# Splitting the projection weights on two engines, and other orders of the lists, in a fused attention and Mamba kernel

## The reference, cut to what matters

```python
# layer 0: cross-attention, 16 heads of 16
q, k, v = relu(x @ Wq + bq), relu(c @ Wk + bk), relu(c @ Wv + bv)
scores = where(mask_of_the_query_row, q k^T / sqrt(16), 1e-9)
x = layernorm(softmax(scores) @ v + x) * gamma + beta
# layer 1, first half: a Mamba block
z, xBC, dt = split(rmsnorm(x) @ in_proj_w)        # 512, 768 and 8 columns
xBC = silu(conv_b + 4 taps along the sequence)    # gives xh (512), B (128), C (128)
dt = softplus(dt + dt_bias); decay = exp(-exp(A_log) * dt)
y = linear recurrence over 128 rows in 8 heads + D_skip * xh
x = x + rmsnorm(y * silu(z)) @ out_proj_w
# layer 1, second half: cross-attention with 8 heads of 32 on the same context
out = x + softmax(layernorm(x) @ Wq1 (c @ Wk1)^T / sqrt(32)) @ (c @ Wv1) @ Wo
```

## Time and profile before

| what | value |
|---|---|
| median of 3 runs | 1336.95 us (1336.31 to 1337.32) |
| the profiled execution | 1338.95 us, of which the span of its trace 1337.2 us |
| mean granted clock of PE | 0.99 |
| PE, DVE, ACT, POOL busy | 97, 90, 85, 69% of the span |
| DMA | 87.00 MB, mean 65 GB/s |
| chain that ended last | PE 87%, DVE 4%, ACT 4%, issue 2% |

### The profile page before, as it was taken

The page is one execution under the profiler, slowest core; times in us unless marked ns, Lnnn a source line. Parts: engine busy times, 40 slices in busy tenths (PEclk is TensorE's granted clock), DMA queues, the critical chain, the costliest instruction groups (busy, mean ns, idle before and its releaser), DMA issues.

```text
span 1337.2 us, 43414 instructions
## 1 busy us (share of the span) xinstructions
PE 1291.6 (97%) x15624; PEld 1148.0 (86%) x15624; DVE 1208.1 (90%) x3056; ACT 1130.8 (85%) x3407; POOL 928.7 (69%) x1200
## 2 busy tenths in 40 slices
PE   5879999999999999999999999999999999999987
PEld 4668889988888998889998889989888898888875
DVE  6789999999999999999999999999999989999982
ACT  5658989888889988888988888998888898888875
POOL 3366777777767777777777776777777777766774
PEclk9889999999999999999999999999999999999999
DMA  6102221212221112222121222211222221111110
GB/s 203 40 34 72 69 77 38 70 56 69 77 77 62 52 49 69 77 77 77 38 66 60 69 77 77 61 53 50 69 77 77 71 71 34 62 56 57 49 57 25
DMA packets 41283, 87.00 MB, mean 65 GB/s; under 512 B 5744, under 2 KB 10992, under 8 KB 41072
## 3 DMA queue, kind: packets, MB, share of 16 engines
q1 hardware_dynamic: 40208, 83.81, 19.7%
...
q10 hardware_dynamic: 864, 0.42, 0.1%
...
## 4 chain that ended last, share of the span: by engine, by line
PE 87%; DVE 4%; ACT 4%; issue 2%; DMA 1%; POOL 1%; SPq 1%; ACTq 0%; DVEq 0%
PE bank L319 26%; PE bank L422 10%; PE bank L550 6%; PE bank L412 5%; PE bank L379 5%; PE bank L533 5%; PE bank L436 4%; PE bank L564 4%; PE bank L669 4%; PE bank L360 3%; PE bank L604 3%; PE bank L625 2%; PE bank L654 2%; PE bank L470 2%; PE bank L416 1%
## 5 line engine op out<-in xcount | busy, mean ns | idle before, releaser
L951 DVE SCALAR_TENSOR_TENSOR ACC<-bank,cw,ACC 128x250 f32<-128x250 f32 (+2 forms) x576 | 264.1, 462 | 5.9 <-ACT ACC L1535 3.3
L319 PE MATMUL bank<-xnT,wnl 128*128 128x256 f32 x640 | 201.6, 315 | 3.3 <-DVE xnL L883 2.3
L1622 ACT ACTIVATE PC<-bank,stc 128x128 f32<-128x128 f32 x512 | 182.5, 389 | 7.7 <-DVE stc L1068 4.3
L319 PE MATMUL bank<-xnL,wnh 128*128 128x256 f32 x640 | 180.3, 282 | 0.0
L319 PE MATMUL bank<-xnT,wnh 128*128 128x256 f32 x640 | 179.8, 281 | 0.0
L800 DVE TENSOR_REDUCE sta<-bank 128x4 f32<-128x512 f32 x256 | 163.7, 673 | 7.8 <-PE bank L379 7.5
L977 DVE TENSOR_TENSOR_SCAN L<-DB,id 128x1024 f32<-128x1024 f32 x64 | 146.8, 2293 | 0.8 <-DMA DB<-dec_scratch 0.8
L319 PEld LDWEIGHTS bank<-xnT,wnl 128*128 128x128 f32 x640 | 121.9, 190 | 26.0 <-issue 17.6
L1437 ACT ACTIVATE PTA<-bank 128x512 f32<-128x512 f32 x256 | 133.3, 628 | 9.0 <-PE bank L416 5.3
L1916 POOL TENSOR_TENSOR PC<-PC,stc 128x512 f32<-128x512 f32 x128 | 132.1, 1042 | 11.3 <-DVE stc L1075 11.3
L319 PEld LDWEIGHTS bank<-xnL,wnh 128*128 128x128 f32 x640 | 122.4, 191 | 0.0
...
## 6 DMA issues: line engine op xcount, KB each, us to landing
...
```

The lines of the kernel that those rows point to most:

```text
L319: mm = e.matmul(t[:, c0:c0 + T], wt[:, k, m:m + 128], x[:, k, :], start=(n == 0), stop=(n == 5))
L951: e.scalar_tensor_tensor(out=w, in0=t[:, 0:T].rearrange("p (b t) -> p b t", b=NB)[:, :, 0:125 + k], scalar=cw[:, c, k:k + 1], in1=w, op0=A ...
L1622: op = e.activation(PC[n % 4][:, p, :], t[:, p * 128:(p + 1) * 128], ACT.Exp, bias=stc[g % 4][:, 4 * i + p:4 * i + p + 1], accum_out=stc[g ...
```

## The change

1. `weights()` becomes `weights(k)`. The half k=0 is done by DVE before `rc(0, 0)`, all of it. For k=1, ACT makes the two wide copies to `wnh` in `eA(0, 4)`; DVE does the rest before `rc(0, 1)`, and waits for ACT's by a new semaphore `z_nk`.
2. ACT's copies `wk1h`, `wv1h` go from `eA(0, 4)` to `n1(0, 1)`, behind `wouth`; POOL's `wk1l`, `wv1l` go from the second call of `xr` to the third (`xr(1, 0)`).
3. The five lists have other orders, in head, loop and tail, and `USES` has other banks. The loops hold the same calls as before; they start at another place of the cycle, and the heads and tails are longer or shorter to match.

```diff
-                    if ns == 0:
-                        weights()
+                    if ns < 2:
+                        weights(ns)
...
-            def weights():
-                e.wait_ge(z_sq, 4)
+            def weights(k):
+                w, wz = pc[:, 4 + k:5 + k], pc[:, 18 + k:19 + k]
                 e.wait_ge(d_win, 32)
-                for k in range(2):
-                    w, wz = pc[:, 4 + k:5 + k], pc[:, 18 + k:19 + k]
+                if k == 0:
+                    e.wait_ge(z_sq, 4)
                     e.tensor_scalar(wnh[:, k, 0:512], stage[k][:, 0:512], wz, None, ALU.mult)
-                    e.tensor_scalar(wnh[:, k, 512:1280], stage[k][:, 512:1280], w, None, ALU.mult).then_inc(z_nh, 1)
...
+                    e.tensor_scalar(wnh[:, k, 512:1280], stage[k][:, 512:1280], w, None, ALU.mult)
+                e.tensor_scalar(wdt[:, k, 1, 0:8], stage[k][:, 1280:1288], w, None, ALU.mult)
+                e.tensor_scalar(wdt[:, k, 0, 0:8], stage[k][:, 1280:1288], w, None, ALU.mult).then_inc(z_nh, 1)
+                e.tensor_scalar(wdt[:, k, 1, 8:16], stage[k][:, 1280:1288], 0.0, None, ALU.mult)
+                e.wait_ge(z_nh, k + 1)
+                if k == 1:
+                    e.wait_ge(z_nk, 2)
+                for lo, hi, c in ((0, 512, wz), (512, 1280, w)):
+                    e.scalar_tensor_tensor(out=wnl[:, k, lo:hi], in0=stage[k][:, lo:hi], scalar=c, in1=wnh[:, k, lo:hi].bitcast(F32),
+                                           op0=ALU.mult, op1=ALU.subtract)
...
                     if n == 4:
-                        e.wait_ge(d_late, 48)
-                        for hi, w in ((wk1h, w1[0]), (wv1h, w1[1])):
-                            e.activation(hi[:, :, :], w, ACT.Copy).then_inc(z_1h, 1)
+                        e.wait_ge(d_win, 32)
+                        for lo, hi, c in ((0, 512, 18), (512, 1280, 4)):
+                            e.activation(wnh[:, 1, lo:hi], stage[1][:, lo:hi], ACT.Copy, scale=pc[:, c + 1:c + 2]).then_inc(z_nk, 1)
...
                             e.activation(wouth[:, k, :], ws[k], ACT.Copy, scale=pc[:, 6 + k:7 + k]).then_inc(z_wo2, 1)
+                        e.wait_ge(d_late, 48)
+                        for hi, w in ((wk1h, w1[0]), (wv1h, w1[1])):
+                            e.activation(hi[:, :, :], w, ACT.Copy).then_inc(z_1h, 1)
...
-                    if ns == 1:
+                    if ns == 2:
```

PE's head up to the first input projection, before and after:

```diff
-            q(0, 0); q(0, 1); k(0, 0); k(0, 1); v(0, 0); sA(0, 0); q(1, 0); q(1, 1); sA(0, 1); tn(0, 0); k(1, 0); v(1, 0)
-            sT(0, 0); k(1, 1); av(0, 0); av(0, 1); av(0, 2); av(0, 3); tn(0, 1); ot(0, 0); q(2, 0); sT(0, 1); q(2, 1)
-            av(0, 4); av(0, 5); av(0, 6); av(0, 7); sA(1, 0); ot(0, 1); sA(1, 1); k(2, 0); v(2, 0); nt(0, 0); cp(0, 0)
...
+            q(0, 0); q(0, 1); k(0, 0); v(0, 0); k(0, 1); sA(0, 0); q(1, 0); q(1, 1); sA(0, 1); k(1, 0); tn(0, 0); v(1, 0)
+            sT(0, 0); av(0, 0); tn(0, 1); av(0, 1); av(0, 2); av(0, 3); k(1, 1); ot(0, 0); q(2, 0); sT(0, 1); q(2, 1)
+            av(0, 4); av(0, 5); av(0, 6); av(0, 7); sA(1, 0); ot(0, 1); sA(1, 1); k(2, 0); nt(0, 0); v(2, 0); cp(0, 0)
```

```diff
-            xc(NG - 1, 4); xc(NG - 1, 5); hm(NG - 2, 1); scan(NG - 1, 0); lg(NG - 1, 0); sz(NG - 1, 1); kk1(NG - 2, 0)
-            kk1(NG - 2, 1); yd(NG - 1, 0); scan(NG - 1, 1); lg(NG - 1, 1); mC(NG - 2, 0); mC(NG - 2, 1); yd(NG - 1, 1)
...
+            scan(NG - 1, 0); lg(NG - 1, 0); kk1(NG - 2, 0); kk1(NG - 2, 1); sz(NG - 1, 1); scan(NG - 1, 1); yd(NG - 1, 0)
+            lg(NG - 1, 1); mC(NG - 2, 0); mC(NG - 2, 1); mC(NG - 2, 2); mC(NG - 2, 3); rC(NG - 2, 0); yd(NG - 1, 1)
...
-            s2_(NG - 1, 0); ga(NG - 1, 1); nC(NG - 2, 0); r2(NG - 1, 0); yl(NG - 1, 1); s2_(NG - 1, 1); nC(NG - 2, 1)
-            lo_u(NG - 1); r2(NG - 1, 1); hr(NG - 1, 0); hr(NG - 1, 1); nC(NG - 2, 2); nC(NG - 2, 3); nC(NG - 1, 0)
...
+            hr(NG - 2, 1); lo_u(NG - 2); xd(NG - 1, 0); dx(NG - 1, 0); xd(NG - 1, 1); ga(NG - 1, 0); dx(NG - 1, 1)
+            yl(NG - 1, 0); s2_(NG - 1, 0); ga(NG - 1, 1); nC(NG - 2, 0); s2_(NG - 1, 1); yl(NG - 1, 1); r2(NG - 1, 0)
+            lo_u(NG - 1); r2(NG - 1, 1); hr(NG - 1, 0); hr(NG - 1, 1); nC(NG - 2, 1); nC(NG - 2, 2); nC(NG - 2, 3)
```

More of the change, by code:

```diff
@@ L288, in sync @@
             e.wait_ge(d_qr, 16)
[L289 to L292, removed]
+            load_x(0); load_c(0); load_m(0); load_x(1); load_c(1); load_x(2); load_t(0); load_m(1); load_c(2); load_m(2)
@@ L293, in sync @@
+            load_t(1); load_x(3); load_x(4); load_m(3); dec_out(0); dec_in(0, 0); load_c(3); load_t(2); load_u(0)
+            dec_in(0, 1); dec_out(1); load_x(5); dec_in(1, 0); load_c(4); load_m(4); load_m(5); load_u(1); load_t(3)
+            dec_in(1, 1); load_x(6); dec_out(2); load_c(5); load_m(6); dec_in(2, 0); dec_in(2, 1); load_t(4); load_u(2)
+            dec_out(3); load_c(6); dec_in(3, 0); store(0)
             for g in range(NG - 9):
-                load_c(g + 6)
-                dec_out(g + 3)
@@ L296, in sync @@
-                dec_in(g + 3, 0)
-                load_m(g + 6)
+                dec_in(g + 3, 1)
+                load_u(g + 3)
+                load_t(g + 5)
                 load_x(g + 7)
[L299 to L309, removed]
@@ L310, in sync @@
-            store(NG - 1)
+                dec_out(g + 4)
+                store(g + 1)
+                load_c(g + 7)
+                load_m(g + 7)
+                dec_in(g + 4, 0)
+            load_x(NG - 2); load_u(NG - 6); dec_in(NG - 6, 1); load_t(NG - 4); load_m(NG - 2); dec_out(NG - 5)
+            load_c(NG - 2); dec_in(NG - 5, 0); load_u(NG - 5); load_x(NG - 1); load_t(NG - 3); dec_in(NG - 5, 1)
+            store(NG - 8); dec_out(NG - 4); store(NG - 7); load_c(NG - 1); dec_in(NG - 4, 0); load_u(NG - 4)
@@ L311, in sync @@
+            dec_in(NG - 4, 1); load_m(NG - 1); load_t(NG - 2); dec_out(NG - 3); dec_in(NG - 3, 0); dec_in(NG - 3, 1)
+            load_t(NG - 1); load_u(NG - 3); load_u(NG - 2); store(NG - 6); dec_out(NG - 2); dec_in(NG - 2, 0)
+            dec_in(NG - 2, 1); store(NG - 5); dec_out(NG - 1); dec_in(NG - 1, 0); dec_in(NG - 1, 1); store(NG - 4)
+            load_u(NG - 1); store(NG - 3); store(NG - 2); store(NG - 1)
             e.wait_ge(d_out[0], 16 * (NG // 2))
@@ new lines, in tensor @@
+            for g in range(NG - 9):
+                y(g + 3, 1)
+                cp(g + 4, 1)
+                o(g + 3, 0)
+                v1(g + 2, 0)
+                cp(g + 4, 2)
+                wp(g + 1, 0)
+                z(g + 4, 0)
+                tn(g + 5, 0)
+                cp(g + 4, 3)
+                o(g + 3, 1)
+                sT(g + 5, 0)
+                cp(g + 4, 4)
+                bd(g + 4, 0)
+                cp(g + 4, 5)
+                av(g + 5, 0)
+                av(g + 5, 1)
+                av(g + 5, 2)
+                av(g + 5, 3)
+                tn(g + 5, 1)
+                tC(g + 2, 0)
@@ L790, in vector @@
+            wp(NG - 1, 0)
         def vector(e):
@@ new lines, in vector @@
+            kk1(3, 0); x2(5, 0); scan(4, 0); rc(5, 1); mA(6, 0); mA(6, 1); xo(5, 1); mA(6, 2); mA(6, 3); bs(5, 1); kk1(3, 1)
+            nm(6, 0); bg(5, 1); lg(4, 0); xs(5, 1); x2(5, 1); nw(6, 0); mA(6, 4); mA(6, 5); yd(4, 0); mA(6, 6); mA(6, 7)
+            scan(4, 1); nl(5, 0); nl(5, 1); mC(3, 0); lg(4, 1); mC(3, 1); mC(3, 2); d0(5, 0); rC(3, 0); d0(5, 1); tap(5, 0)
+            yd(4, 1); tap(5, 1); tap(5, 2); tap(5, 3)
+            for g in range(NG - 9):
+                rC(g + 3, 1)
+                r1(g + 4, 0)
+                dc(g + 5, 0)
+                tap(g + 5, 4)
+                dc(g + 5, 1)
+                xc(g + 5, 0)
+                dc(g + 5, 2)
+                mC(g + 3, 3)
+                hh(g + 4, 0)
+                tap(g + 5, 5)
+                dc(g + 5, 3)
+                dc(g + 5, 4)
+                dc(g + 5, 5)
+                tap(g + 5, 6)
+                hs(g + 4, 0)
+                fin(g + 2, 0)
+                dc(g + 5, 6)
+                hg(g + 4, 0)
+                xc(g + 5, 1)
+                rC(g + 3, 2)
+                dc(g + 5, 7)
+                rC(g + 3, 3)
+                nm(g + 6, 1)
+                dc(g + 5, 8)
+                sz(g + 5, 0)
+                dc(g + 5, 9)
+                tap(g + 5, 7)
+                dc(g + 5, 10)
+                tap(g + 5, 8)
+                nw(g + 6, 1)
+                r1(g + 4, 1)
```

685 lines of the change are left out of this document (310 added, 375 removed), and 22 rows, old and new, of the table USES.

## The result

The changed kernel takes 1340.62 us (median of 20 runs, 1336.22 to 1348.21), the kernel before 1338.17 us (median of 20, 1336.31 to 1341.78; the three runs shown ahead had 1336.95). The ratio is 1.0023, 95% interval 1.0014 to 1.0032: slower, by a little more than the 0.2% that can be told from nothing. The forecast was 1331.0, or 1332.2 against the median of 20. All ratios leave out the slow runs, of which there were two: one of 4303.87 us in run 11, and one of 1436.88 us of the kernel before, measured beside runs 8, 10 and 11. The profiled execution of after took 1341.28 us with a span of 1339.5: 2.3 more than the one of before, so the pair of traces shows about the same loss.

A forecast was written before the change was run, and what follows sets the result against it. PE was taken as the bound, full in the middle, with 45 us idle at the ends. Head 5.5 plus tail 1.3 less loop 0.8 gave 6.0 us: 1336.95 to 1331.0, range 1325.5 to 1339.5.

The forecast's parts named there:

- The hole of 3.15 us and the chain to `cp(0, 0)`: Head: splitting weights() starts sT(0, 1) 3.0 us earlier, near 28.9, and cp(0, 0) at 43.7 instead of 48.20.
- Head, -5.5: First 140 us: 4.5 us by cp(0, 0) plus 1.0 at gm(0, 0); bounds 1.5 and 10.
- the 1.0 at `gm(0, 0)`: Head: of PE's 3.40 us wait at 77.71 us, 1.0 gained, bounds 0 and 2.4.
- Rival B: Head's gain is taken up behind it, as DVE's work sets 55 to 90 us; 1334 to 1337 us, chance 0.17.
- Loop, +0.8: Turned order of the loop's lists costs 0.03 us a group, 0.8 in all; bounds -1 and +10.
- The sentence that failed is the one on SP: Loop: load_c and load_m pass dec_in; each has most of a group's time, and DMA share is 0.21.
- `cp(g, 5)` in bank 6: Loop: closest new pair, behind sT(g, 0), freed by the first eA; slack 0.05 to 0.1 us.
- `sT(g, 0)` in bank 5: Loop: now waits on sz(g, 0), a tanh and a product within 2.4 us; some 0.9 left.
- Rival C: New wait in each group, cp(g, 5) on a late eA; 0.35 us a group, about 1341 us, chance 0.13.
- Tail, -1.3: Tail: the last r2 on POOL comes at 1308.8 instead of 1310.1 us; bounds -2 and +4.
- the last group's path after that is the same: Tail behind the last r2: softmax, transposes, output projection and store were taken as unchanged.
- 0.12 for slower: Chance given to the changed kernel measuring slower than before; faster had 0.72, same 0.16.

The follow-up runs named there:

- run 11: Kernel of run 10 with the loop's store, load_c and load_m on SP moved behind dec_in(g + 4, 0); 1333.27 us, ratio 0.9954.
- run 8: The changed kernel once more, unaltered, for a second profile; 1337.83 us in its one run.
- run 10: db_apart with part of the old tail put back, and split_c(3) and lo_c(3) moved earlier in the head; 1331.59 us, ratio 0.9942.
- db_pair: Kernel before, with dec_in(g + 3, 1) issued directly behind dec_in(g + 3, 0) on SP; 1338.96 us, ratio 1.0004.
- sp_in_before: Kernel before, with the changed kernel's order on SP: store, load_c and load_m ahead of both dec_in, issued together; 1343.63 us, ratio 1.0042.
- runs 6 and 7: 6: kernel before with only the weights split and its copy moves, 1336.21 us. 7: db_apart with these taken back, new orders kept, 1339.79 us.
- db_apart: Changed kernel with dec_in(g + 3, 1) put behind load_u(g + 3) on SP, so the two broadcasts go out apart; 1333.62 us, ratio 0.9966.

## Why the prediction was wrong

- **The hole of 3.15 us and the chain to `cp(0, 0)`**: right in kind. The hole goes in all six profiles, and from `sT(0, 0)` to `sT(0, 1)` it is 6.5 us in each, for 9.7 before (9.2 in db_pair and sp_in_before, which keep the old head). That the forecast was met to 0.4 us at `sT(0, 1)` and to 0.0 at `cp(0, 0)` is luck: the other five are 1.5 to 1.9 and 1.6 to 2.7 us later, and the two holes behind changed otherwise than I said. That both were needed for it, the split and the new orders, I had not seen: runs 6 and 7 have one each, and `cp(0, 0)` at 47.88 and 51.97.
- **Head, -5.5**: the size is right, the make-up is not. Six profiles of this head put the scan of group 3 at 183.4 to 187.0, so 3.6 to 7.2 us early, 4.7 in the mean (the old head has it at 190.3 to 191.5 in three profiles). Of this, idle time is only 1.7 in the profile of after (28.5 to 26.8); the rest goes with the clock (0.96 for 0.91), on which the forecast itself counted 1.5 at most. Of the 1.0 at `gm(0, 0)` I was wrong in kind: that wait went, and one of 4.71 us for `lo_c(3)` stands at `k(3, 0)` in its stead. Rival B described this stage well (run 10: DVE sets it), but the clock moved more than the waits did.
- **Loop, +0.8**: this is the step that failed; it was 8.7 us in the profile of after and 2.2 in the second. The bounds (-1 to +10) held both, but I put the weight on the mild end and looked for the danger in the wrong place. `cp(g, 5)` in bank 6 and `sT(g, 0)` in bank 5 never waited in the loop. The sentence that failed is the one on SP: `load_c` and `load_m` pass `dec_in`, "each has most of a group's time, and the DMA share is 0.21". I asked whether the passing transfers had time, and not whether the one that was passed had it: `dec_in` is issued behind a wait of its own, some 6 us before the scan, and needed 3.7 of them. A mean share of 0.21 says nothing of the 6 us in which everything goes out at once. Nor did I count `dec_in(g + 3, 1)` moving next to it, nor that `ht(g, 0)` now takes its bank from the maximum behind the scan. Rival C had the price (10.5 for 8.7) and the point (0.35 us a group), by another mechanism: a near hit by luck. Taking its cause away gave 1333.62, 0.9966: the forecast's direction, and 4.7 of its 6 us (1338.35 in the same comparison).
- **Tail, -1.3**: right at an equal clock, and spoilt in the profile of after. From the scan of group 30 to the end it is 81.9 us before and 80.4 in the second profile and in db_apart, all three with a clock of 0.94 behind the last `r2`: a gain of 1.5. In the profile of after it is 82.2, with 0.83 there. From group 30 to the last `r2` 2.0 us are gained (54.4 before, 52.4 after), and 0.3 to 0.5 are lost behind it, since "the last group's path after that is the same" was false: `nC(30, 1)`, which I let go behind `r2`, had to be done there. What I had not looked at is the stretch before: from group 24 to group 30 the new lists take 235.3 to 236.6 us (after, run 8, db_apart), for 234.7 before, and that eats most of the gain. Why is open.
- **Sum**: -7.2 + 8.7 + 0.8 = +2.3 in the profiled pair, and -3.7 + 2.2 + 0.3 = -1.2 with the second profile, for -5.5 + 0.8 - 1.3. A range that ended at 1339.5, with 0.12 for slower, was too narrow for a loop whose lists all turn.
